# Router logits of the first stage with the gate weights stationary in four column groups

## The reference

```
# stage 0: a conditional mix of the 64 rows of a batch, then a gated layer with sign weights
att   = softmax(mlp(cond))                               # (32, 8)
y     = einsum('boi,bih->boh', att-mix of weight, x) + agg_b
logits  = y @ gate_w.T                                   # (2048, 8)
routing = softmax(logits)
x1 = x + (y * (routing @ in_scale)) @ sign(W).T * (routing @ out_scale) + bias
# stage 1: grouped convolution over channels, then a linear layer with an attention over 8 LoRA experts
z  = conv1d(x1) + ctx
out = x1 + z @ W1.T + b + sum_e softmax(q.k)_e * (z A_e) B_e
```

## Time and profile before

| | |
|---|---|
| median of three runs | 617.22 us |
| profiled execution, first to last instruction | 617.4 us |
| stage 0, up to the last L429 (about) | 248.6 us |
| TensorE busy | 591.4 us (96%) |
| DVE, ACT, POOL busy | 252.3, 113.5, 147.0 us |
| L391, matmuls (256 records) | 31.1 us |
| L391, weight loads (256 records) | 32.7 us |

### The profile page before, as it was taken

One profiled execution on the slowest core, in us unless ns is written; L12 is line 12 of the kernel. 1 busy time (PEld: TensorE's weight loads), 2 busy tenths in 40 slices (PEclk: granted clock), 3 DMA queues, 4 the chain that ended last, 5 costly groups with the idle time before them and its releaser, 6 DMA issues.

```text
span 617.4 us, 9165 instructions
## 1 busy us (share of the span) xinstructions
PE 591.4 (96%) x3381; PEld 516.5 (84%) x3381; DVE 252.3 (41%) x479; ACT 113.5 (18%) x255; POOL 147.0 (24%) x79
## 2 busy tenths in 40 slices
PE   4799999999999999999999999999999999999997
PEld 3677878778787878988988988988988998998996
DVE  4547766666775655623123123123123123123122
ACT  4522222222222213301101101101101101101100
POOL 0324345453444344801101101101101101101100
PEclk9769999999997999999999999999999999999999
DMA  9903242332323348512311312311321321321100
GB/s 291 355 1 112 89 140 102 108 110 72 110 84 98 112 131 188 141 63 45 107 70 37 106 71 35 106 72 34 106 74 32 106 75 31 106 78 28 69 35 34
DMA packets 36110, 58.15 MB, mean 94 GB/s; under 512 B 4096, under 2 KB 24384, under 8 KB 36096
## 3 DMA queue, kind: packets, MB, share of 16 engines
q1 hardware_dynamic: 35952, 57.70, 30.0%
q10 hardware_dynamic: 144, 0.26, 0.1%
HBM read 41.15 MB, written 16.79 MB: 94 GB/s over the span
## 4 chain that ended last, share of the span: by engine, by line
PE 89%; DVE 4%; ACT 1%; issue 0%; DVEq 0%
PE bank L498 47%; PE bank L429 17%; PE bank L480 9%; PE bank L391 4%; PE bank L382 4%; PE bank L526 4%; DVE gate L762 3%; PE bank L405 2%; PE bank L411 1%; PE bank L397 1%; ACT gate L601 1%; DVE routing L768 0%; DVE routing L766 0%; DVE gate L756 0%; DVE gate L758 0%
## 5 line engine op out<-in xcount | busy, mean ns | idle before, releaser
L498 PE MATMUL bank<-early,parts 128*128 128x320 f32 (+1 forms) x1152 | 206.5, 337 | 0.0
L498 PEld LDWEIGHTS bank<-early,parts 128*128 128x128 f32 x1152 | 184.7, 188 | 15.7
L429 PE MATMUL bank<-late,parts 128*128 128x512 f32 x512 | 140.6, 420 | 0.7 <-ACT parts L610 0.7
L429 PEld LDWEIGHTS bank<-late,parts 128*128 128x128 f32 x512 | 97.3, 200 | 22.9 <-issue 4.2
L935 POOL TENSOR_TENSOR work<-work,bias_bc 128x1024 f32<-128x1024 f32 x16 | 38.7, 2422 | 285.8 <-DMA work<-x_scratch 285.8
L498 PE MATMUL bank<-late,parts 128*128 128x512 f32 x384 | 93.9, 393 | 0.0
L498 PEld LDWEIGHTS bank<-late,parts 128*128 128x128 f32 x384 | 70.9, 188 | 15.8
L903 POOL TENSOR_TENSOR work<-work 128x512 f32<-128x512 f32 x32 | 40.8, 1276 | 80.4 <-DVE work L790 80.4
L480 PE MATMUL bank<-band,raw 128*128 128x128 f32 x512 | 59.7, 275 | 0.0
L480 PEld LDWEIGHTS bank<-band,raw 128*128 128x128 f32 x512 | 59.0, 192 | 0.1
L610 ACT ACTIVATE parts<-work 128x512 fp32r<-128x512 f32 x64 | 40.0, 633 | 74.8 <-DVE work L827 43.7
(11 more groups left out here) (90 smaller groups left out, 363.5 us busy)
## 6 DMA issues: line engine op xcount, KB each, us to landing
xs<-in_x SPq DMA_DIRECT2D x16, 512.0 KB, 3.7
x_scratch<-work SPq DMA_DIRECT2D x16, 512.0 KB, 2.9
raw<-x_scratch SPq DMA_DIRECT2D x128, 64.0 KB, 3.1
work<-x_scratch SPq DMA_DIRECT2D x16, 512.0 KB, 3.6
out_tokens<-work SPq DMA_DIRECT2D x15, 512.0 KB, 2.7
stage<-in_wearly SPq DMA_DIRECT2D x8, 576.0 KB, 3.8
row_bc<-token_rows_scratch SPq DMA_DIRECT2D x30, 64.0 KB, 3.6
work<-in_wsign SPq DMA_DIRECT2D x3, 512.0 KB, 12.6
```

The source lines that it names most:

```text
L429: last = mm(bank[4 + h][:, :], parts[:, p, a, c, :], signs[:, c, h * HALF:(h + 1) * HALF], start=(k % 16 == 0), stop=(k % 16 == 15))
L498: return mm(dst, parts[:, p, a, c, :], w(b, c), start=(k == 0), stop=(close and k == 23))
```

## The change

`consts` now holds the gate weights of each chunk padded from 8 to 32 columns (256 columns of the table in place of 64) and a selection matrix `C_SEL` of 8 columns, which has a 1 where the row number modulo 32 is the column number. `product_logits` takes the gate weights as the stationary operand and the y chunk, 128 tokens wide, as the moving one. Chunk c writes to the 32 partitions of group c % 4 in bank 0; chunks c and c + 4 add up there. ACT copies that 128 x 128 result to SBUF (`copy_logits`), and one more product (`sum_logits`) takes it as the stationary operand and the selection as the moving one: it adds the four partial sums and brings the tokens to the partitions, into bank 2 as before. `product_logits` stands at k = 12 as before, the sum at k = 15, the turn at 21 and the scales at 25. The wait for `u_ready`, which guards bank 2, moves with the sum.

```diff
-C_GATE, C_ID = 362, 426
-C_END = 554
+C_GATE, C_ID = 362, 618
+C_SEL = 746
+C_END = 754
+EP = 32
-LOGITS_AT, TURN_AT, SCALES_AT, CONV0_AT = 12, 20, 24, 8
+LOGITS_AT, SUM_AT, TURN_AT, SCALES_AT, CONV0_AT = 12, 15, 21, 25, 8
...
             def product_logits(i, p):
                 for c in range(L8):
                     if c % 4 == 0:
                         pe.wait_ge(y_biased, 4 * i + 2 * p + 1 + c // 4)
-                    last = mm(bank[2][:, 0:E], y_t[:, c, :], cst[:, C_GATE + c * E:C_GATE + (c + 1) * E],
-                              start=(c == 0), stop=(c == L8 - 1))
-                last.then_inc(logits_done, 1)
+                    at = slice(EP * (c % 4), EP * (c % 4) + EP)
+                    last = mm(bank[0][at, 0:P], cst[:, C_GATE + c * EP:C_GATE + (c + 1) * EP], y_t[:, c, :],
+                              start=(c < 4), stop=(c >= 4))
+                last.then_inc(logits_made, 1)
+
+            def sum_logits(i, p):
+                pe.wait_ge(logits_copied, 2 * i + p + 1)
+                mm(bank[2][:, 0:E], logits_t[:, :], cst[:, C_SEL:C_SEL + E], start=True, stop=True).then_inc(logits_done, 1)
...
             product_logits(0, 0)
+            sum_logits(0, 0)
...
                     if k == LOGITS_AT:
+                        product_logits(ni, q)
+                    if k == SUM_AT:
                         pe.wait_ge(u_ready, 4 * i + 2 * p + 2)
-                        product_logits(ni, q)
+                        sum_logits(ni, q)
...
+            def copy_logits(i, p):
+                act.wait_ge(logits_made, 2 * i + p + 1)
+                do(logits_t[:, :], bank[0][:, 0:P], ACT.Copy).then_inc(logits_copied, 1)
...
             def tile0(i, p, reused=True, fresh=False):
+                copy_logits(i, p)
                 gate_exps(i, p)
```

More of the change, by code:

```diff
@@ L101, in adaln_ffn_kernel @@
         gate = sb("gate", [P, 64])
+        logits_t = sb("logits_t", [P, P])
         qk = sb("qk", [P, 2, NQK // 2])
@@ L162, in adaln_ffn_kernel @@
         y_biased = sem("y_biased")
+        logits_made = sem("logits_made")
+        logits_copied = sem("logits_copied")
         logits_done = sem("logits_done")
@@ L964, in lay_out @@
     consts[:, C_B1] = f["L0_cond_b1"]
-    consts[:, C_GATE:C_GATE + L8 * E] = turned(f["L0_ffn_gate_w"]).reshape(P, L8 * E)
+    consts[:, C_GATE:C_ID].reshape(P, L8, EP)[:, :, 0:E] = turned(f["L0_ffn_gate_w"])
+    consts[:, C_SEL:C_SEL + E] = np.arange(P)[:, None] % EP == np.arange(E)[None]
     consts[:, C_ID:C_ID + P] = np.eye(P, dtype=np.float32)
```

## The result

The changed kernel took 624.87 us (median of 4 runs, 624.15 to 627.37) beside 617.46 us of the kernel before on the same chip: ratio 1.0124, 95% interval 1.0102 to 1.0146. It is slower by 1.2%, some 7.4 us. Forecast were 617.8, with a range up to 624.0; the measured time lies above the range. The profiled execution spans 625.6 us, against 617.4. A run's time is 1.8 us longer than its span (627.37 for 625.6), so the profile shows the slowest of the four runs, and that of the kernel before, at about 619.2, lies 0.3% above its median and not 0.03%; both may hold a fall of the clock more than a median run. The mean granted clock was 0.959 in the profiled run of the changed kernel and 0.962 to 0.967 in its other three.

The account below looks back on a forecast made before the run. A loop through TensorE, DVE and POOL, its division held by POOL, was taken as the bound. Steady part 0, constants +0.3, first tile +0.3, second +0.1, last period -0.2: +0.5 us on 617.4, forecast 617.8, range 613.0 to 624.0.

Parts of the forecast that it names:

- the overlap of the groups: New logits products on TensorE: only neighbouring passes overlap, 1.05 us per period; 0.43 with four groups side by side, 1.70 with none.
- What bounds the kernel: Steady periods: a closed loop through TensorE, DVE and POOL, 13.99 us into even turns, 12.67 into odd; TensorE's saving becomes waiting.
- Falls as many as before, within one: Steady part: loop unchanged and about two falls of TensorE's clock, as before; 615.5 to 619.6 us, chance 0.48.
- The rival that was written for this case: Steady part: longer TensorE waits bring three more clock falls at a mean of 2.2 us; about 623 us, chance 0.20.
- The other half of rival 1: Seam between two POOL instructions: DVE's division would pass there, gaining at most 0.45 us per even period, 3 in all.
- The copy: ACT's copy of the logits: 0.28 us, about 0.35 with hand-overs, hidden behind large products, so the sum does not wait: 0.
- The switches of the array: TensorE, each period: changing the array's layout and back costs 0.2 us, ends 0 and 0.4.
- The start: Before the steady periods: +0.3 us for the larger constants, +0.3 for the first tile, +0.1 for the second.
- The last period: Last period of stage 0: the large product that moved ahead of the turn saves its 0.235 us, taken as -0.2.

Follow-up runs that it names:

- e4: Changed kernel with the exponentials and quotients kept in PSUM in place of SBUF; 592.17 us, ratio 0.9599 to the kernel before.
- e6: Kernel before, old logits product, with the exponentials and quotients kept in PSUM in place of SBUF; 600.30 us, ratio 0.9741 to the kernel before.
- e8: Changed kernel with four extra large products, result unused, on TensorE directly ahead of the turn in even periods; 615.46 us, ratio 0.9976 to the kernel before.
- e2: Changed kernel with all eight logits chunks in one column group, the selection taking those rows alone; 618.33 us, ratio 1.0019 to the kernel before.
- e9: Changed kernel with only the exponentials in PSUM, the quotients staying in SBUF; 620.24 us, ratio 1.0068 to the kernel before.
- e3: Kernel before with two of the eight chunks of the logits product, so its routing is another; 626.81 us, ratio 1.0168 to the kernel before.
- e1: Changed kernel with eight extra large products, result unused, on TensorE directly ahead of the turn in even periods; 613.09 us, ratio 0.9934 to the kernel before.
- e5: Kernel before with five extra large products, result unused, directly ahead of the turn in even periods; 613.77 us, ratio 0.9952 to the kernel before.
- e7: Kernel before with the constants table as wide as in the changed kernel, none of the new products; 618.01 us, ratio 1.0019 to the kernel before.

## Why the prediction was wrong
The time is above the range. Two steps failed: the overlap of the groups was taken at 1.05 us and was 0.57, and the falls of the clock, which the sum had at nothing, cost 11.5 us. By its steps:

- **What bounds the kernel: right.** The loop turn, L405, DVE, POOL, L762 held by L895, turn was the bound, and TensorE's saving turned into waiting: even stretches of 13.94 to 14.04 us before and 13.99 to 14.01 after. e4 and e6 show it by removing the hold.
- **The overlap of the groups: mis-sized, and this is where the forecast left the road.** It took 1.05 us on the argument that the two passes of one product follow each other in the queue. They took 0.57: in the trace the first four matmuls start 7 ns apart, and there are four such rounds, about 0.11 us one after the other; the second pass of a chunk does not keep the next three chunks from starting. Net per period that is TensorE about -0.8 rather than -0.24, read from the even waits (2.15 less 1.36, with the turns as far apart as before); the waits follow: 2.15 in place of the forecast 1.8 at even turns, 0.82 in place of 0.5 at the odd turn that no fall preceded.
- **"Falls as many as before, within one": failed.** There were 6 in place of 2, at 2.67 us in place of 2.2. That is +11.5 us in the steady part, where the sum had 0. The rival that was written for this case took three more falls and gave 623; with four more and their measured price it would have given 617.4 + 11.5 less what the start gained. It had a chance of 0.20 because five of seven waits had had no fall. What e8, e2 and e9 show is that the kernel before stood at the edge: waits of 0.9 us gave no fall, 1.3 us gave 2, 1.9 to 2.2 us gave 6. The forecast itself added 0.45 us of waiting at each even turn and still left the number of falls as it was, without a row for it; no run has even waits of its 1.8 us. The other half of rival 1, a division that passes at the seam, did not come: the even divisions started 0.05 to 0.09 us too late for it, and only e3 shows it.
- **The copy: right.** It cost 0.28 us, and the steady sums had no wait for it.
- **The switches of the array: near.** Behind the last logits matmul the next large one comes after 0.20 us, as part of the 0.57; 0.2 for both sides was taken. In e2, too, it is 0.20 us, where passes follow each other at 0.11. The side ahead can't be read apart from the loads.
- **The start: wrong in sign.** Forecast +0.7 up to the second tile, measured -3.4. The first turn is later by 0.24 us (23.42, 23.18), where +0.6 was forecast; the second comes at 38.88 in place of 42.00. The windows show TensorE's clock: in the kernel before it stood at 0.5 from 22.3 to 42.8 us, in the changed one it was back at 1.0 from 29.8 to 33.2 and again from 36.7. All kernels with the new logits product, e2 with one group too, had it back by 37.5, those with the whole old one at 41.0 to 43.1; e3, with a quarter of the old one, at 34.5. So it goes with the logits product; why is open, for it was not tested apart.
- **The last period, +0.1 in place of -0.2:** within what such small terms can be read to.

## What to carry to other kernels
A busy share of 96% and 89% of the chain did not make TensorE the bound: compare its work with the length of the loop that releases it, and ask where a saving would go before making it. Where it would become a wait on TensorE, it can cost more than it saves: here waits of 1.36 us that grew to 2.15 came with six falls of the clock in place of two. Filling the wait with products whose result nobody reads is a fair test, and a stopgap worth 1.9% here. The cure is to end the wait itself, here small instructions of DVE, 8 to 32 elements wide, held by a long one of POOL; with their operands in PSUM they were not held, and the same change then made the kernel faster by 1.5%.

## What the runs showed of the hardware
- With four column groups, 16 fp32 passes of 128 columns held TensorE for 0.57 us, in one group (e2) for 1.87.
- Waits of TensorE of 0.9 us and less, followed by a transposition and four large products, brought no fall of the clock in 35 even turns (e1, e2, e4, e5, e6); of 1.27 to 1.42 us, 6 in 21 (before, e7, e8); of 1.9 to 2.2 us, 12 in 14 (the changed kernel, e9); of 2.5 us, 5 in 5 (e3). This is one profiled execution of each. A fall lasted 3.4 or 6.8 us, once 10.2 (e3), and in the changed kernel and e8 it cost 1.2 to 3.2 us.
- Between two POOL instructions that stand back to back a waiting DVE instruction passed (e3: the division ended at 46.76, the first POOL instruction at 46.74), and the next DVE instruction was held by the second one (until 49.07; it ended at 49.04). In e3 this was so in six of the seven even periods.
- Moving the input of these small DVE instructions, or input and output, to PSUM took the hold away: the division took 0.22 to 0.24 us in all 16 tiles (e4, e6, e9), where it had taken up to 2.3.
